# The output projection of an attention kernel as three products of rounded parts

## Time and profile before

| | |
|---|---|
| Time, median of 3 runs | 1502.11 us (1501.95 to 1503.66) |
| The profiled execution's own time | 1502.1 us |
| Its span | 1500.3 us |
| Mean granted TensorE clock | 0.967 |
| PE busy | 1390.5 us, 93% |
| PEld busy | 1144.7 us, 76% |
| DVE busy | 994.2 us, 66% |
| ACT busy | 963.8 us, 64% |
| POOL busy | 758.2 us, 51% |

### The profile page before, as it was taken

How to read it: one execution, slowest core, us unless ns; L and a number is a source line. 1 busy time by engine, 2 the same in 40 slices (tenths; PEclk the granted TensorE clock), 3 DMA queues, 4 the chain that set the end, 5 groups by cost and what they waited for, 6 DMA issues and landing times.

```text
span 1500.3 us, 37780 instructions
## 1 busy us (share of the span) xinstructions
PE 1390.5 (93%) x10823; PEld 1144.7 (76%) x10823; DVE 994.2 (66%) x4355; ACT 963.8 (64%) x2992; POOL 758.2 (51%) x1520
## 2 busy tenths in 40 slices
PE   2572999999999999999999999799999999999997
PEld 1231788888888888878999999688888888888886
DVE  4677677777777777772222221288888888888886
ACT  1121777777777777775454545387777777777775
POOL 1241566676776667660000000167777666777764
PEclk8695999999999999999999999899999999999999
DMA  9775666666666666645666666567676666767662
GB/s 284 269 247 176 188 177 194 183 180 186 187 189 183 185 190 183 183 128 180 210 192 212 200 204 200 150 189 193 184 193 188 180 185 172 194 186 192 188 177 66
DMA packets 441412, 283.00 MB, mean 189 GB/s; under 512 B 18666, under 2 KB 415508, under 8 KB 441236
## 3 DMA queue, kind: packets, MB, share of 16 engines
q1 hardware_dynamic: 433044, 264.12, 61.1%
q0 software_dynamic: 8192, 16.79, 3.9%
HBM read 135.01 MB, written 145.77 MB: 187 GB/s over the span
## 4 chain that ended last, share of the span: by engine, by line
PE 86%; DVE 5%; SPq 3%; DMA 2%; issue 2%; POOL 1%; ACT 1%; DVEq 0%; ACTq 0%; POOLq 0%
PE ps L1420 14%; PE ps L1440 12%; PE ps L1345 9%; PE ps L1309 9%; PE ps L1310 9%; PE ps L1311 9%; PE ps L1450 9%; PE ps L1409 8%; PE ps L1380 4%; PE ps L1327 1%; DMA skew<-gst 1%; SPq L400 1%; DMA wproj<-in_L_attn_Wproj_dram 1%; DMA xn_d<-xn 1%; SPq L453 1%
## 5 line engine op out<-in xcount | busy, mean ns | idle before, releaser
L810 ACT ACTIVATE prob<-logit,low 128x128 f32<-128x128 f32 x1024 | 403.6, 395 | 232.1 <-DVE low L1120 230.0
L1120 DVE CUSTOM_DVE_ANT_0 logit<-ps,extra 128x128 f32<-128x128 f32 x1024 | 256.4, 288 | 190.8 <-PE ps L1420 179.8
L676 POOL TENSOR_SCALAR prob<-prob,inv 128x128 f32<-128x128 f32 x512 | 189.0, 369 | 237.1 <-DVE inv L1106 233.4
L1420 PE MATMUL ps<-qk 64*128 64x256 f32 (+1 forms) x2048 | 237.7, 351 | 2.2 <-DVE low L1120 2.2
L1420 PEld LDWEIGHTS ps<-qk 64*128 64x128 f32 x2048 | 177.4, 187 | 78.7 <-issue 33.7
L1094 DVE TENSOR_TENSOR probT<-ps,keep 128x256 f32<-128x256 f32 x512 | 214.0, 418 | 26.6 <-PE ps L1409 25.7
L1409 PE MATMUL ps<-ident,prob 128*128 128x128 f32 x1024 | 200.5, 279 | 0.4 <-POOL prob L678 0.3
L1440 PE MATMUL ps<-probT,val 128*64 128x256 f32 (+1 forms) x2048 | 194.7, 332 | 5.4 <-DVE probT L1095 5.4
L810 ACT ACTIVATION_READ_ACCUMULATOR prob<-logit,low 128x1 f32 x1024 | 191.1, 187 | 0.0
L651 POOL CAST r_hi<-r_raw 120x512 fp32r<-120x512 f32 x64 | 39.6, 618 | 297.5 <-ACT r_raw L773 297.4
L678 POOL TENSOR_SCALAR prob<-prob,inv 128x128 f32<-128x128 f32 x512 | 186.9, 365 | 0.0
(11 more groups left out here) (179 smaller groups left out, 2792.2 us busy)
## 6 DMA issues: line engine op xcount, KB each, us to landing
skew<-gst SPq DMA_DIRECT2D x384, 256.0 KB
extra<-skew SPq DMA_DIRECT2D x256, 256.0 KB, 3.4
w1b<-w_d SPq DMA_DIRECT2D x39, 514.0 KB, 3.5
w2b<-w_d SPq DMA_DIRECT2D x39, 320.0 KB, 3.3
x_place<-zero SPq DMA_DIRECT2D x39, 256.0 KB, 2.8
placed<-x_place SPq DMA_DIRECT2D x39, 256.0 KB, 3.7
y_place<-yrow SPq DMA_DIRECT2D x39, 256.0 KB, 2.2
w_d<-w1s SPq DMA_DIRECT2D x1, 4112.0 KB, 11.9
```

The source lines that it names most:

```text
L676: nc.gpsimd.tensor_scalar(prob[:, h, 0:P], prob[:, h, 0:P], inv[:, h, 0:1], 1.0, ALU.mult, ALU.mult).then_inc(norm_made, 1)
L810: ins = nc.scalar.activation(prob[:, h % PB, a:b], logit[:, h % LB, a:b], ACT.Exp, scale=-1.0, bias=low[:, h % LB, t:t + 1], accum_out=tot ...
L1120: ins = nc.vector.tensor_tensor_reduce(out=logit[:, h % LB, a:b], in0=ps[:, S_BANK[n], a:b], in1=extra[:, h, a:b], scale=1.0, scalar=BIG, ...
L1420: mm = nc.tensor.matmul(ps[:, S_BANK[n], cols], qk[rows, pair % 2, 0, q], qk[rows, pair % 2, 1, k], start=True, stop=True)
```

## The change

Wproj is loaded into wproj_r and split in the preparation: ScalarE makes wproj_hi with a copy of 128x1024, VectorE makes wproj_lo with a subtraction of the same size, between the split of brev and the reciprocal rstd. In the sequences ScalarE's copy now writes head_hi (rounded) in place of headT, and VectorE makes head_lo as the bank minus head_hi: a new step `low_heads` in odd slots, placed behind the reciprocals and ahead of the sums L1120. `outputs` waits for head_low and calls `product`: twelve float32r matmuls of 128 columns in place of four float32 calls.

```diff
@@ build, tiles
-        wproj = sb("wproj", [P, PAIRS, E])
+        wproj_hi = sb("wproj_hi", [P, PAIRS, E], F32R)
+        wproj_lo = sb("wproj_lo", [P, PAIRS, E], F32R)
...
+        wproj_r = sb("wproj_r", [P, PAIRS, E])
...
-        headT = sb("headT", [P, 2, T])
+        head_hi = sb("head_hi", [P, 2, T], F32R)
+        head_lo = sb("head_lo", [P, 2, T], F32R)
@@ ScalarE, preparation, behind the wqk_hi copies
+            nc.scalar.copy(wproj_hi[:, :, :], wproj_r[:, :, :]).then_inc(wproj_split, 1)
...
+            act.wait_ge(wproj_split, 2)
             for e in range(NX):
                 prep_copy(FIRST["w1"] + e, w1s[:, e, 0:FF], bank(FIRST["w1"] + e))
@@ ScalarE, sequence, even slots
-                        nc.scalar.copy(headT[:, :, :].rearrange("p n t -> p (n t)"),
-                                       ps[:, HEAD_BANK, :]).then_inc(head_made, 1)
+                        nc.scalar.copy(head_hi[:, :, :].rearrange("p n t -> p (n t)"),
+                                       ps[:, HEAD_BANK, :]).then_inc(head_high, 1)
@@ VectorE, preparation, ahead of rstd
+            dve.wait_ge(wproj_split, 1)
+            nc.vector.tensor_tensor(wproj_lo[:, :, :], wproj_r[:, :, :], wproj_hi[:, :, :].bitcast(F32), ALU.subtract
+                                    ).then_inc(wproj_split, 1)
             dve.wait_ge(std_ready, 1)
@@ VectorE, sequence
                         nc.vector.reciprocal(inv[:, h:h + 2, :], total[:, h:h + 2, :]).then_inc(inv_made, 1)
+                    if j % 2 == 1 and here(i, j - 5, heads, start):
+                        low_heads(i, (j - 5) // 2)
                     if heads:
...
+            def low_heads(i, quad):
+
+                dve.wait_ge(head_high, i * QUADS + (quad + 1))
+                wait_from(dve, out_psum, i * QUADS + quad)
+                nc.vector.tensor_tensor(head_lo[:, :, :].rearrange("p n t -> p (n t)"), ps[:, HEAD_BANK, :],
+                                        head_hi[:, :, :].bitcast(F32).rearrange("p n t -> p (n t)"),
+                                        ALU.subtract).then_inc(head_low, 1)
@@ TensorE, outputs
-                pe.wait_ge(head_made, i * QUADS + (quad + 1))
+                pe.wait_ge(head_low, i * QUADS + (quad + 1))
                 for t in range(2):
+                    rows = slice(t * P, (t + 1) * P)
                     for pair in range(2):
-                        mm = nc.tensor.matmul(ps[:, HEAD_BANK, t * E:(t + 1) * E],
-                                              headT[:, pair, t * P:(t + 1) * P],
-                                              wproj[:, (2 * quad + pair) % PAIRS, :],
-                                              start=(pair == 0), stop=(pair == 1))
+                        k = (2 * quad + pair) % PAIRS
+                        mm = product(ps[:, HEAD_BANK, t * E:(t + 1) * E], ((head_hi[:, pair, rows], head_lo[:, pair, rows]),
+                                                                          (wproj_hi[:, k, :], wproj_lo[:, k, :])),
+                                     start=(pair == 0), stop=(pair == 1))
                 mm.then_inc(out_psum, 1)
```

More of the change, by code:

```diff
@@ L257, in build @@
         wr_split = sem("wr_split")
+        wproj_split = sem("wproj_split")
         brev_split = sem("brev_split")
@@ L323, in build @@
         head_psum = sem("head_psum")
-        head_made = sem("head_made")
+        head_high = sem("head_high")
+        head_low = sem("head_low")
         out_psum = sem("out_psum")
@@ L411, in _ @@
             sp.dma_start(wv_r[:, :], Wv).then_inc(attn_in, 16)
-            sp.dma_start(wproj[:, :, :], Wproj.rearrange("(k d) e -> d k e", d=P)).then_inc(attn_in, 16)
+            sp.dma_start(wproj_r[:, :, :], Wproj.rearrange("(k d) e -> d k e", d=P)).then_inc(attn_in, 16)
             sp.wait_ge(prep_made, FIRST["small"])
```

## The result

The changed kernel takes 1620.7 us, the median of 4 runs (1615.65 to 1623.43), against 1502.61 (1501.95 to 1503.66): the ratio is 1.078, with a 95% interval from 1.0755 to 1.0807. Forecast were 1619 us; the prediction gives 1590 to 1650 as the forecast's own range and takes it down to 1560. The profiled execution has a span of 1621.7 us, 121.4 more than before.

A forecast was written before the change was run, and what follows sets the result against it. TensorE, busy for 93% of the span, was taken as the bound. Longer calls 57, waits 59 and preparation 1 sum to 117 us on 1502.1, giving 1619 us, with its own range 1590 to 1650, down to 1560 including one rival.

The forecast's parts named there:

- TensorE bound in attention, so work and waits count in full: In attention TensorE is busy 495.87 of 500 us, so every microsecond of added work or wait counts in full.
- Step of a 128-column float32r matmul, 0.112, from its load: In `outputs`, each float32r matmul was taken as bound by its weight load at 0.112 us, above 59 ns of streaming.
- +57: Longer `outputs` calls on TensorE, twelve matmuls for eight: 0.45 us more in each of 128 calls, 57 us.
- The waits, +59: TensorE's waits ahead of `outputs` for VectorE's subtraction, worked out slot by slot over 128 calls: 59 us in all.
- gains nothing in slots 5 and 7: VectorE was said not to get ahead in slots 5 and 7, the gap before `outputs` being made anew each time.
- The call near the end that I put at 2.4: One `outputs` call near the end, its reciprocal far behind, was given a wait of about 2.4 us.
- 0.74 us for a call: In both halves' drains, six calls directly following ScalarE's copy get the subtraction whole, 0.69 + 0.05 us each, 4.4 in all.
- VectorE no bound at 67% busy: The 128 subtractions add 88 us to VectorE, leaving it about 67% busy over the span, so no bound.
- Preparation, +1: Before attention, the 128x1024 subtraction costs 1 us, with ends of nothing and twice 1.22; ScalarE's wproj copy is covered.
- hidden waits (1564): Rival: waits ahead of `outputs` are hidden, only drains and longer calls count, 1564 us; chance 0.11.
- Faster loads (1543 or 1488): Rival: float32r loads at the transposes' rate; 1543 us with waits, chance 0.06, or 1488 with the drains' 4 alone, 0.03.
- Short matmuls at the float32 rate (1791): Rival: 128-column float32r matmuls in `outputs` go like float32, a call takes 2.69 us, total 1791; chance 0.09.

The follow-up runs named there:

- experiment 1: Changed kernel without VectorE's subtraction, the third product taking head_hi for head_lo, TensorE waiting only for ScalarE's copy: 1557.97 us, ratio 1.037.
- experiment 2: Kernel before with its four float32 products, plus VectorE's subtraction and TensorE's wait for it: 1559.21 us, ratio 1.037.
- (5): Changed kernel with each of the twelve matmuls of a call moving 64 columns in place of 128: 1643.35 us, ratio 1.092.
- (6): Changed kernel with 8 loads and matmuls per call for 12, same columns streamed, VectorE adding the bank's halves in two steps: 1572.64 us, ratio 1.048.
- experiment 3: Kernel before plus a subtraction of the same size at the same place on VectorE, for which nobody waits: 1515.76 us, ratio 1.009.
- (10): Kernel before with outputs moved behind their slot's transposes and the addition behind the second copy of probabilities, nothing else: 1498.15 us, ratio 0.996.

## Why the prediction was right

- **TensorE bound in attention, so work and waits count in full:** right. Experiments 1 and 2 cost their whole sums, and together they give the growth of each half within 0.4 us.
- **Step of a 128-column float32r matmul, 0.112, from its load:** right; 0.11 with 128 and with 64 columns (5), and 8 loads bring the call to 0.97 (6). What was off is the overhead: I took 8 loads at 0.112 and 0.10 to get going, and let the 0.10 stand for twelve; the call went from 1.00 to 1.39, which is 12 x 0.111 and 0.06, so +50 and not +57. Beside the clock, which the working left out, this was the largest error of the sum.
- **The waits, +59:** measured by the distance from the logits over 124 calls, and from the transposes or values ahead of the last two calls of each half, calls start 59 us later too, but this is made up otherwise than I worked it out. By slot it is 0.52 for 0.56, 0.56 for 0.60 and 0.91 for 0.95, all 0.04 short because the subtraction takes 0.66 us and not 0.69. Slot 5 of the second half has 0.52 for 0.65: VectorE, late there before, had gained. I had said that it gains nothing in slots 5 and 7, and by that step I was wrong for this one. The calls needn't be longer for it: in experiment 2, with its short calls, it is 0.52 too. The call near the end that I put at 2.4 waits 1.2. What made up for all this are the drains. I had 0.74 us for a call; the last but one of each half has 1.8 and 1.5, since there the subtraction stands behind the copies of probabilities, and the last has 2.0, of which 0.73 are the subtraction and 1.3 are the values ahead of it, which took 2.83 us for 1.52 at the low clock. I had left both out.
- **VectorE no bound at 67% busy:** right for the changed kernel (66%), wrong as a reason. The mean hides the second half; experiment 3 costs 12.6 us with the same subtractions and short calls. That the longer calls are what gave it room is read from the shares (328 of 400 us for 351), not tested.
- **Preparation, +1:** the subtraction takes 1.21 us, directly ahead of the reciprocal; attention started 1.5 later. That isn't clear of noise: experiment 1 has the same subtraction and starts attention 0.4 later, experiment 2 hasn't and starts it 0.5 earlier.

```profile
55.75 1.21 DVE L953 TENSOR_TENSOR wproj_lo<-wproj_r,wproj_hi 128x1024 fp32r<-128x1024 f32 x1
```

- **The rivals:** hidden waits (1564) are out by the idle time under head_lo. Faster loads (1543 or 1488) are out: the loads take 194 to 196 ns. The rule of the Trainium skill, page TensorE: Matmul & The Clock Gate, section Weight-path perf modes, says that the fast weight load is on for 128 weights of another type than FP32. The cheap loads that I drew from it aren't borne out by these float32r weights, whose loads take as long as the float32 ones with 191; the same table counts no win for fp32. Short matmuls at the float32 rate (1791) are out by the call of 1.39.

The sum came within 2 us of the median, closer than its terms: +50 for the calls, +59 for the later starts, +1.5 for the preparation, and some 7, mostly of the clock in the drains and at the start of the experts, that the working didn't have, against 7 too many for the calls. The mechanism was right in its main parts; that the errors cancel to 2 us is luck.

## What to carry to other kernels

Count weight loads, not columns: a product split in three costs three loads where plain float32 costs two, and with 128 columns moving the load is the step here, 0.11 us for 0.06 of streaming. A copy between engines that was free because it ended early isn't free any more when a second engine is put behind it in an ordered list; read the gap between its last possible end and its reader slot by slot, and if it is negative, try the reader behind other work first (47 us here). And test two remedies together: each frees time that the next engine in line needs, as VectorE did here.

## What the runs showed of the hardware that I had not expected

- The granted clock fell to 0.50 (1.2 GHz) in the first drain and in the first sequence, where TensorE sat idle for 1 to 3 us again and again between short pieces of work; at that level the step of the twelve loads is 0.21 us in place of 0.11, and a load takes up to 339 ns where the median is 192, so loads slow down with the clock too.
- Taking half of the streamed columns out of one call in attention (5), with all waits and loads as they were, brought the clock down to 0.87 to 0.96 in nine of 14 stretches of the second half, and the kernel took 23 us more than the changed one, which has 1.00 in all 14.
- The same float32 call of eight matmuls holds TensorE for 1.00 us between logits with 64 rows of weights and transposes, and for 0.81 between transposes and keys (10). Which of the neighbours matters wasn't tested.
